# Attention block on one core: late tiles in seven half-size jobs in place of four, and split key and query parts stored by feature

## The reference, cut to what matters

```
mod = silu(c) @ wmod                      # sa, ca, ga, sb, cb, gb
h = layernorm(x) * (1 + ca) + sa
q, k, v = split(h @ W_attn)               # 16 heads of 16
att = softmax(where(causal, q k^T / 4, -inf)) * decay(i - j)
x = x + ga * ((att @ v) @ W_proj)
h = layernorm(x) * (1 + cb) + sb
x = x + gb * (h @ (W + up_aux lora_up lora_down down_aux)^T + b)
```

## Time and profile before

| | us |
|---|---|
| median of 3 runs | 1386.57 (1386.45 to 1388.49) |
| the profiled execution | 1388.68 |
| its span, first to last instruction | 1386.6 |
| ACT busy | 1271.8 (92%) |
| PE busy | 1238.1 (89%) |
| DVE busy | 958.3 (69%) |
| POOL busy | 273.2 (20%) |
| first exponential of stage 2 | 119.04 |

### The profile page before, as it was taken

How to read it: one execution, slowest core, us unless ns; L and a number is a source line. 1 busy time by engine, 2 the same in 40 slices (tenths; PEclk the granted TensorE clock), 3 DMA queues, 4 the chain that set the end, 5 groups by cost and what they waited for, 6 DMA issues and landing times.

```text
span 1386.6 us, 29414 instructions
## 1 busy us (share of the span) xinstructions
PE 1238.1 (89%) x11211; PEld 761.1 (55%) x11211; DVE 958.3 (69%) x2110; ACT 1271.8 (92%) x2624; POOL 273.2 (20%) x615
## 2 busy tenths in 40 slices
PE   7935999999999999999999999999999998888786
PEld 5612555656565655656565555656565554544443
DVE  4634777777777777777777777777777776655554
ACT  2635999999999999999999999999999999999995
POOL 0001111404031231403122141403121020303030
PEclk9977999999999999999999999999999999999999
DMA  4575110011112101111112001111112000010100
GB/s 152 229 241 161 24 30 18 25 37 30 32 40 73 32 14 30 28 38 30 32 31 81 17 25 31 30 37 30 28 28 77 17 10 23 13 28 17 28 1 17
DMA packets 114180, 64.68 MB, mean 47 GB/s; under 512 B 79323, under 2 KB 110834, under 8 KB 114034
## 3 DMA queue, kind: packets, MB, share of 16 engines
q1 hardware_dynamic: 112306, 62.36, 15.2%
q10 hardware_dynamic: 1728, 0.39, 0.1%
HBM read 41.74 MB, written 20.97 MB: 45 GB/s over the span
## 4 chain that ended last, share of the span: by engine, by line
PE 52%; ACT 17%; DVE 13%; issue 5%; ACTq 0%; DVEq 0%
PE fast_s_ps L1016 20%; ACT fast_s_ps L1283 11%; PE fast_t_ps L1073 9%; PE fast_t_ps L1042 8%; PE fast_t_ps L1058 7%; ACT fast_probs L1283 6%; DVE fast_negmax L1386 4%; DVE fast_probsT L1405 4%; PE fast_t_ps L1104 3%; PE fast_t_ps L1155 1%; PE fast_s_ps L1025 1%; DVE fast_probsT L1395 1%; PE fast_t_ps L1084 1%; DVE fast_y_sb L1424 1%; PE fast_t_ps L1147 1%
## 5 line engine op out<-in xcount | busy, mean ns | idle before, releaser
L1283 ACT ACTIVATE fast_s_ps<-fast_s_ps,fast_negmax 128x1024 f32<-128x1024 f32 (+4 forms) x768 | 812.9, 1073 | 19.4 <-PE fast_s_ps L1016 17.6
L1016 PE MATMUL fast_s_ps<-k_stack,xq 96*128 96x512 bf16 (+3 forms) x2448 | 655.6, 354 | 78.6 <-DMA xq<-parts_d 37.1
L1283 ACT ACTIVATE fast_probs<-fast_s_ps,fast_negmax 128x640 f32<-128x640 f32 (+7 forms) x512 | 456.8, 892 | 35.8 <-DVE fast_negmax L1386 34.4
L1395 DVE TENSOR_TENSOR fast_probsT<-fast_t_ps,fast_dec_c 128x384 f32<-128x384 f32 (+2 forms) x512 | 276.3, 540 | 191.7 <-PE fast_t_ps L1042 190.2
L1386 DVE TENSOR_REDUCE fast_negmax<-fast_s_ps 128x1 f32<-128x512 f32 (+3 forms) x512 | 339.2, 662 | 95.9 <-PE fast_s_ps L1025 93.6
L1016 PEld LDWEIGHTS fast_s_ps<-k_stack,xq 96*128 96x128 bf16 x2448 | 210.6, 98 | 300.9 <-ACT fast_s_ps L1283 70.1
L1042 PE MATMUL fast_t_ps<-ident,fast_probs 128*128 128x128 f32 x1488 | 252.1, 276 | 32.7 <-DVE fast_y_sb L1424 15.5
L1042 PEld LDWEIGHTS fast_t_ps<-ident,fast_probs 128*128 128x128 f32 x1488 | 179.0, 141 | 93.9 <-DVE fast_y_sb L1424 22.6
L1405 DVE TENSOR_TENSOR fast_probsT<-fast_t_ps,fast_dec_c 128x256 f32<-128x256 f32 x464 | 191.9, 414 | 11.9 <-PE fast_t_ps L1058 0.5
L1283 ACT ACTIVATION_READ_ACCUMULATOR fast_s_ps<-fast_s_ps,fast_negmax 128x1 f32 x768 | 199.2, 259 | 0.0
L1058 PE MATMUL fast_t_ps<-ident,fast_probs 128*128 128x128 f32 x912 | 188.5, 287 | 10.4 <-DVE fast_probsT L1405 2.1
(11 more groups left out here) (161 smaller groups left out, 766.0 us busy)
## 6 DMA issues: line engine op xcount, KB each, us to landing
k_stack<-parts_d SPq DMA_DIRECT2D x96, 128.0 KB, 2.8
xq<-parts_d SPq DMA_DIRECT2D x372, 32.0 KB, 2.1
parts_d<-part SPq DMA_DIRECT2D x15, 512.0 KB, 3.4
fast_vals<-v_d SPq DMA_DIRECT2D x36, 128.0 KB, 2.4
parts_d<-k_stack SPq DMA_DIRECT2D x72, 64.0 KB, 1.7
xb<-x_dram SPq DMA_DIRECT2D x32, 128.0 KB, 2.1
out_dram<-xb SPq DMA_DIRECT2D x32, 128.0 KB, 2.0
xq<-x_dram SPq DMA_DIRECT2D x5, 512.0 KB, 4.8
```

Of the source, the lines that this page charges most:

```text
L1016: return nc.tensor.matmul(s_ps[:, n % SLOTS, at:at + w], q, k_stack[:, h, k0:k0 + w], start=True, stop=stop)
L1283: nc.scalar.activation(dst, src, ACT.Exp, bias=negmax[:, p % 2, side, h:h + 1], scale=-1.0, accum_out=sums[:, p % 2, side, h, c:c + 1]).th ...
L1395: nc.vector.tensor_tensor(probsT[:, turned(side, s), 0:n, :], t_ps[:, 0:P * n].rearrange("p (b q) -> p b q", q=P), dec_c[:, WIN - nb:WIN - ...
```

## The change

It does four things.

1. `parts_d` becomes [part, group, keys or queries, feature, token] in place of [part, group, partition, m, token]. The weights' columns are taken in the order of parity (`by_parity`), so that the partition p of block m holds feature 2p + m, and a partition's two rows lie next to each other in `parts_d`. A store of a part in stage 1 writes rows of 2 KB in place of 4 KB. DVE scales the weights with three instructions for each half in place of two, two of them with a stride of 2 in the source.
2. `load_keys` needs one transfer of 16 partitions by 16 heads by 512 tokens, 256 KB, for each pair, so 6 for a group in place of 12. The query loads keep their count and size.
3. Each late tile has seven jobs in place of four. Keys, queries and values are cut in two, of 4 matmul instructions and a read of 128 columns each (two instructions of DVE for keys and queries, one for values).
4. Their steps: first tile 3, 5, 7, 9, 11, 13, 14; others -1, 1, 3, 5, 7, 11, 13; last -1, 1, 3, 5, 7, 9, 11 (in the order of `LATE_KINDS`).

```
-    parts_d = nc.dram_tensor("parts_d", [PARTS, NG, P, 4, GT], bf16, kind="Internal").ap()
+    parts_d = nc.dram_tensor("parts_d", [PARTS, NG, 2, C, GT], bf16, kind="Internal").ap()
+    KEYS, QUERIES = 0, 1
...
-                    for m in range(2):
-                        eng.dma_start(k_stack[rows_of(j), QH * m:QH * (m + 1), g * GT:(g + 1) * GT],
-                                      parts_d[kp, g, :, m, :].rearrange("(h d) t -> d h t", d=HD)).then_inc(done, 16)
+                    eng.dma_start(k_stack[rows_of(j), :, g * GT:(g + 1) * GT],
+                                  parts_d[kp, g, KEYS].rearrange("(h d) t -> d h t", d=HD)).then_inc(done, 16)
...
+            def by_parity(columns):
+                return columns.rearrange("p (n m) -> p m n", m=2)
...
-                    sp.dma_start(parts_d[n, g], part[n][:]).then_inc(part_stored[n][g % 2], 16)
+                    sp.dma_start(parts_d[n, g].rearrange("a (p m) t -> p a (m t)", m=2), part[n][:].rearrange("p (a m) t -> p a (m t)", m=2)).then_inc(part_stored[n][g % 2], 16)
...
-                    step(nc.vector.tensor_scalar(wa_s[:, 3 * cc, :], wa[:, cc, 0:C], mod_c[:, SCALE_A, cc:cc + 1],
-                                                 SCORE_SCALE, ALU.mult, ALU.mult))
-                    step(nc.vector.tensor_scalar(wa_s[:, 3 * cc + 1:3 * cc + 3, :],
-                                                 wa[:, cc, C:3 * C].rearrange("p (a c) -> p a c", c=C),
-                                                 mod_c[:, SCALE_A, cc:cc + 1], None, ALU.mult))
+                    step(nc.vector.tensor_scalar(wa_s[:, 3 * cc, :].rearrange("p (m n) -> p m n", m=2), by_parity(wa[:, cc, 0:C]),
+                                                 mod_c[:, SCALE_A, cc:cc + 1], SCORE_SCALE, ALU.mult, ALU.mult))
+                    step(nc.vector.tensor_scalar(wa_s[:, 3 * cc + 1, :].rearrange("p (m n) -> p m n", m=2),
+                                                 by_parity(wa[:, cc, C:2 * C]), mod_c[:, SCALE_A, cc:cc + 1], None, ALU.mult))
+                    step(nc.vector.tensor_scalar(wa_s[:, 3 * cc + 2, :], wa[:, cc, 2 * C:3 * C],
                                                  mod_c[:, SCALE_A, cc:cc + 1], None, ALU.mult))
...
+            LATE_KINDS = ("x_turn", "keys0", "keys1", "queries0", "queries1", "values0", "values1")
+            FIRST_STEPS = (3, 5, 7, 9, 11, 13, 14)
+            LATE_STEPS = (-1, 1, 3, 5, 7, 11, 13)
+            LAST_STEPS = (-1, 1, 3, 5, 7, 9, 11)
...
-                LATE_AT[s0 - 1 if s0 > 0 else 3] = ("x_turn", r)
-                LATE_AT[s0 + 5] = ("keys", r)
-                LATE_AT[s0 + 7] = ("queries", r)
-                LATE_AT[s0 + 11] = ("values", r)
+                steps = FIRST_STEPS if s0 == 0 else LAST_STEPS if r == len(LATE_TILES) - 1 else LATE_STEPS
+                for kind, h in zip(LATE_KINDS, steps):
+                    LATE_AT[s0 + h] = (kind, r)
...
-                            for k in range(2):
-                                m = k if kind == "keys" else 2 + k
-                                for cc in range(CH):
-                                    last = nc.tensor.matmul(t_ps[:, P * k:P * (k + 1)], kq_weights(cc, m), l_hT[:, cc, :],
-                                                            start=(cc == 0), stop=(cc == CH - 1))
+                            m = LATE_KINDS.index(kind) - 1
+                            for cc in range(CH):
+                                last = nc.tensor.matmul(t_ps[:, 0:P], kq_weights(cc, m), l_hT[:, cc, :],
+                                                        start=(cc == 0), stop=(cc == CH - 1))
...
-                            nc.vector.tensor_tensor(l_kq[k], src, bias, ALU.add).then_inc(late_sum, 1)
-                            nc.vector.tensor_tensor(l_part[0][:, 2 * k:2 * k + 2, :], src, bias, ALU.add).then_inc(turn_free, 1)
+                            bias = kq_bias[:, m:m + 1].to_broadcast([P, P])
+                            nc.vector.tensor_tensor(l_kq[m // 2][:, m % 2, :], t_ps[:, 0:P], bias, ALU.add).then_inc(late_sum, 1)
+                            nc.vector.tensor_tensor(l_part[0][:, m, :], t_ps[:, 0:P], bias, ALU.add).then_inc(turn_free, 1)
```

More of the change, by code:

```diff
@@ L272, in load_queries @@
             for j, (qp, _) in enumerate(PAIRS):
-                rows = parts_d[qp, i // G, :, 2 + half, P * (i % G):P * (i % G + 1)]
+                rows = parts_d[qp, i // G, QUERIES, P * half:P * (half + 1), P * (i % G):P * (i % G + 1)]
                 sp.dma_start(q_stack[rows_of(j), u % 2, side, :, :],
@@ L931, in store_late @@
                             if n == 0:
-                                sp.wait_ge(turn_free, late_job_no(("keys", "queries")[k], r) + 1)
+                                sp.wait_ge(turn_free, late_job_no(("keys1", "queries1")[k], r) + 1)
                             else:
                                 sp.wait_ge((late_mid, late_low)[n - 1], 2 * r + k + 1)
-                            sp.dma_start(parts_d[n, t // G, :, 2 * k:2 * k + 2, P * (t % G):P * (t % G + 1)],
-                                         l_part[n][:, 2 * k:2 * k + 2, :]).then_inc(late_parts_stored, 16)
+                            rows = parts_d[n, t // G, k, :, P * (t % G):P * (t % G + 1)]
+                            sp.dma_start(rows.rearrange("(p m) q -> p m q", m=2), l_part[n][:, 2 * k:2 * k + 2, :]).then_inc(late_parts_stored, 16)
                     def store_late_v(r):
                         t = LATE_TILES[r]
-                        sp.wait_ge(turn_free, late_job_no("values", r) + 1)
+                        sp.wait_ge(turn_free, late_job_no("values1", r) + 1)
                         sp.dma_start(v_d[t // G, :, t % G, :], l_v).then_inc(late_v_stored, 16)
@@ L946, in stack_late_keys @@
                         sp.wait_ge(late_v_stored, 16 * (r + 1))
-                        sp.wait_ge(turn_full, late_job_no("values", r) + 1)
+                        sp.wait_ge(turn_full, late_job_no("values1", r) + 1)
                         for n in range(PARTS):
@@ L1178, in weight_job @@
                         last.then_inc(tail_full, 1)
-                    pe.wait_ge(k_loaded, 32 * len(PAIRS) * K_EARLY)
+                    pe.wait_ge(k_loaded, 16 * len(PAIRS) * K_EARLY)
                     for s in range(NSTEP):
@@ L1338, in late_split @@
                         high, mid_part, low = (part[:, 2 * k:2 * k + 2, :] for part in l_part)
-                        pool.wait_ge(turn_free, late_job_no(("keys", "queries")[k], r) + 1)
-                        pool.wait_ge(late_sum, n)
+                        pool.wait_ge(turn_free, late_job_no(("keys1", "queries1")[k], r) + 1)
+                        pool.wait_ge(late_sum, 2 * n)
                         nc.gpsimd.tensor_tensor(l_kq[k], l_kq[k], high, ALU.subtract).then_inc(late_rest, 1)
@@ L1483, in late_out @@
                             nc.vector.tensor_copy(l_hT, t_ps[:, 0:C].rearrange("p (c q) -> p c q", c=CH)).then_inc(turn_free, 1)
-                        elif kind == "values":
-                            if r > 0:
+                        elif kind in ("values0", "values1"):
+                            o = P * ("values0", "values1").index(kind)
+                            if r > 0 and o == 0:
                                 dve.wait_ge(late_v_stored, 16 * r)
-                            nc.vector.tensor_tensor(l_v, t_ps[:, 0:C], v_bias, ALU.add).then_inc(turn_free, 1)
+                            nc.vector.tensor_tensor(l_v[:, o:o + P], t_ps[:, 0:P], v_bias[:, o:o + P], ALU.add).then_inc(turn_free, 1)
                         else:
-                            k = ("keys", "queries").index(kind)
-                            if r > 0 and k == 0:
+                            m = LATE_KINDS.index(kind) - 1
+                            if r > 0 and m == 0:
                                 dve.wait_ge(late_low, 2 * r)
                                 dve.wait_ge(late_parts_stored, LATE_STORES * r)
-                            src = t_ps[:, 0:C].rearrange("p (m q) -> p m q", m=2)
-                            bias = kq_bias[:, 2 * k:2 * k + 2].unsqueeze(2).to_broadcast([P, 2, P])
-                            nc.vector.tensor_tensor(l_kq[k], src, bias, ALU.add).then_inc(late_sum, 1)
-                            nc.vector.tensor_tensor(l_part[0][:, 2 * k:2 * k + 2, :], src, bias, ALU.add).then_inc(turn_free, 1)
+                            bias = kq_bias[:, m:m + 1].to_broadcast([P, P])
+                            nc.vector.tensor_tensor(l_kq[m // 2][:, m % 2, :], t_ps[:, 0:P], bias, ALU.add).then_inc(late_sum, 1)
+                            nc.vector.tensor_tensor(l_part[0][:, m, :], t_ps[:, 0:P], bias, ALU.add).then_inc(turn_free, 1)
                     def late_rows(s):
```

15 lines of the change are left out of this document (8 added, 7 removed).

## The result

| | before | after |
|---|---|---|
| median | 1388.04 us (14 runs, 1386.45 to 1390.43) | 1392.90 us (14 runs, 1389.52 to 1396.54) |
| profiled execution | 1388.68, span 1386.6 | 1390.13, span 1388.0 |
| first exponential | 119.04 | 114.11 |
| pairs 0 to 11 | 942.97 | 949.09 |

The ratio is 1.0033, 95% interval 1.0021 to 1.0045: the change makes the kernel slower by 4.9 us. 1390.6 was forecast against 1386.57, which is 4.0 more. The sum came out; its two terms, +12.5 us for the pairs with a late tile and -8.5 us for the transfers of stage 1, did not. The rest of this document is about that. "The pairs" are pairs 0 to 11 throughout, and a "half" is one of the six half-size jobs of a late tile.

A forecast was written before the change was run, and what follows sets the result against it. The prediction took PE's queue to bound pairs with a late tile, and the key transfers the end of stage 1. +12.5 - 8.5 = +4.0 us put the median at 1390.6 us, range 1382 to 1400.

The forecast's parts named there:

- +12.5 us for the pairs: Stage 2, pairs with a late tile: half jobs cost nearly a whole hand-over, +12.5 us, bounds +4 and +19.
- -8.5 us for the transfers: End of stage 1: larger key transfers start the first scores earlier, -8.5 us, bounds +1.5 and -14.
- an odd step's half costs its hand-over: PE's queue in late pairs: a keys or queries half costs 0.94 us, a values half 0.89, PE waiting for DVE's reads.
- Pair 0: +0.9 forecast: First pair of stage 2, halves at steps 5, 7, 9, 11, 13 and 14 beside the weight work: +0.9 us.
- All of it shows: Late pairs: PE's lead over ACT hides none of the added +1.31 us a pair.
- (a): SP's key issues from 67.57, ahead of the store ACT waits for: 3.0 us earlier, bounds 0 and 4.
- (b): SP's 24 key issues from 84.41, limited by the DMA engines after the change: 5.2 us earlier, bounds 0 and 8.3.
- (c): Six key issues from 104.03 become three, the last store queued behind: 1.1 us earlier, bounds 0 and 1.9.
- full is about 304 GB/s: Stage 1 key loads: fully busy DMA engines would move about 304 GB/s, from 204 GB/s at 0.67 busy.
- The +0.8 us set against it: Stage 1: part stores in 2 KB rows and DVE's extra, strided weight scaling cost +0.8 us, bounds 0 and 1.5.
- the 5 to 8 us: By the skill's rule the issue stays at 0.6 us and the 24 key issues from 84.41 save 5 to 8 us.
- The late keys stall nothing: Ends of pairs 3 and 7: later key loads fit with some 2 us; rival, pairs 4 and 8 stall 2 us each, chance 0.05.

The follow-up runs named there:

- `even7`: The changed kernel with the six half jobs of a late tile moved to even steps; 1372.74 us, ratio 0.988.
- `keys_only`: The kernel before with only the new layout and the six larger key transfers a group, four full late jobs kept; 1387.21 us, ratio 0.9989.
- `jobs_only`: The kernel before with only the seven late jobs, over the old layout and twelve key transfers a group; 1396.4 us, ratio 1.0051.
- `no13`: The changed kernel with the halves of every late pair at steps 5, 7, 9, 11, 13 and 14; 1528.5 us, ratio 1.0999.
- `from3`: The changed kernel with the halves at steps 3, 5, 7, 9, 11 and 13, pair 0 as it is; 1392.36 us, ratio 1.0026.

## Why the prediction came out, point by point

- **PE's queue sets the pace of a late pair, and an odd step's half costs its hand-over.** Right: 0.90 for 0.94, 0.78 for 0.89 (values), `turn_back`'s wait stayed whole. `even7` shows the second part: the same jobs, with the hand-over covered, take 20.6 us less.
- **+12.5 us for the pairs.** Measured +6.1, inside the bounds of 4 and 19, but half. The terms that failed: (1) The pieces were 0.04 (four keys and queries halves) and 0.11 (two values halves) too dear, the latter because I put all of `bn_aggr` in front of the read: 0.38 a pair, 4.2 us over eleven pairs. Small errors in a price that is paid six times a pair are two thirds of the gap. (2) Pair 0: +0.9 forecast, -0.4 measured; steps 5 and 7 gave back 0.72 each. (3) "All of it shows" was read from pair 3 alone. In pair 7 steps 3 and 13, taken with the even step behind each, grew by 0.48 and 0.61 only, since PE's even steps are 4.44 there, not 4.60, and ACT had paced them; PE's row in step 3 of pair 7, before, is below. Pairs 5 to 7 came out 0.7 to 0.9 under my figure, 0.4 of it by (1). With (1) and (2) that makes about the gap of 6.4. One pair stood for eleven.

```profile
686.67 0.39 PE L1016 MATMUL fast_s_ps<-k_stack,xq 96*128 96x512 bf16 x1 [0.51 <-ACT fast_probs L1283]
```

- **-8.5 us for the transfers.** Measured -2.6 (116.47 against 119.04 at the same clock). Its parts, `keys_only` against before: (a) the twelve keys start at 83.52 for 84.41, 0.9 for 3.0, because the store that ACT waits for was issued 5.0 us earlier (71.32 for 76.33) but landed only 0.9 earlier (78.78 for 79.71); (b) from there to the landing of the high store 18.68 for 19.61, 0.9 for 5.2; (c) from there to the last query 12.61 for 13.36, 0.75 for 1.1. The issue time was right, 0.65 us at twice the size. The step that failed is "full is about 304 GB/s", worked out by scaling 204 GB/s with a busy share of 0.67. Measured with almost only keys: 223 to 245, of which the keys some 200. The +0.8 us set against it had no row behind it: in `keys_only` DVE's six scaling instructions take 0.35 us each, strided or not, 2.1 in place of 1.7; what the 2 KB rows of the stores cost no run separates.
- The Trainium skill (DMA: Bandwidth & Descriptors, section Anatomy of one DMA) was cited for many descriptors at little cost. That section describes transfers issued by GpSimd, and SP issued these; the issue time agrees all the same, 0.65 us for twice the rows; the 5 to 8 us that I attached to it do not, since the landing, not the issue, became the limit: 5.4 us to landing for 2.8.
- **The late keys stall nothing.** Right after the change; with twelve issues (`jobs_only`) the same delay costs 1.0 us, so the larger transfers pay there too.
- **The signs.** Steps 1, 3, 5, 7 and 13 of pair 3 were to be 5.64, 5.80, 4.74, 5.17 and 5.07; they are 5.66, 5.67, 4.71, 5.14 and 5.01, the pair 79.6 for 80.0. ACT's idle time behind steps 1 and 3 was to be near 0.9 and is 0.79 and 0.69. PE's first score matmul was to be near 109 and is at 112.6, an issue 0.85 and takes 0.65, the DMA share near 1 and is 1.1, at a lower rate than I gave it.
- **The total.** The errors of 6.4 and 5.9 us have opposite signs and cancel. The forecast of +4.0 is right in sum (3.8 at equal clock) by luck. The profiled executions alone differ by 1.4 us, since that of before held 2.4 us more at the lower clock: one profile of each would have been misread.

## What to carry to other kernels

Price an inserted job by what stands behind it in the same buffer: 0.90 us of queue where the next user waits for the reader, 0.34 where 0.8 us of other matmuls lie between. Then ask which engine's queue its follow-up work sits in, and who waits behind that: the halves two steps later (`no13` against `from3`) cost 136 us. And before you add up a change over many rounds, price the piece in the cheapest and the dearest round, over as many steps as a lead lasts; don't turn a busy share into a rate that no row has shown.

## What the runs showed of the hardware

- A DMA issue of 16 partitions by 16 rows of 1 KB takes 0.61 (median) to 0.65 us (back to back), as one of 8 rows (0.60 to 0.67); the landing goes from 2.8 to 5.4 us.
- The busy share of the DMA engines isn't proportional to what they move: 0.67 at 204 GB/s and 1.13 to 1.16 at 223 to 245 GB/s with almost only 1 KB rows of keys, but 1.04 at 327 GB/s with 4 KB rows of stores among them. The keys' 1 KB rows moved 198 to 204 GB/s in all four stretches.
- TensorE is at its lower level for some 3.4 us, near 25 us and in pairs 13 to 15, in some executions of the same program: 2.4 us in stage 1, 1.1 us in a pair's step. The mean clock of the executions of after falls from 0.985 to 0.978 as they go from 1390 to 1396.5 us.
